# Four cross-attention layers in one kernel: recurrent read-outs and group-norm root on GpSimd, the tail of the grouped-query stage moved into the next stage, and weights loaded in another order

## The chip, the cores and the metric

One core of one Trainium2 chip runs the whole program; the other cores are idle. The metric is the device time of one launch in microseconds (us). The engines are TensorE (PE), VectorE (DVE), ScalarE (ACT), GpSimd (POOL) and SyncE (SP), which issues nearly all DMAs. Every engine runs a program of its own, written out by hand, and they meet only at semaphores.

## What is computed

Four layers in a row work on `x`, 4 batches of 256 tokens by 256 channels in f32, against a context of the same shape. Cut to what matters here:

```python
# L0: 16-head cross attention with a gate, then a layer norm on its input side
# L1: recurrent layer, 32 heads of 8 channels
def step(s, inp):
    k_l, v_l, w_l, r_l = inp
    a = k_l[..., :, None] * v_l[..., None, :]
    out = einsum('bhs,bhst->bht', r_l, faaaa * a + s)      # the read-out
    return a + w_l[..., None] * s, out
_, outs = lax.scan(step, s0, seq)
y = outs.transpose(1, 0, 2, 3)
gm = mean(y, -1); gv = mean((y - gm) ** 2, -1)             # group norm over 8 channels
y = ((y - gm) * rsqrt(gv + EPS)).reshape(B, L, C) * gn_w + gn_b
x = x + y * g @ Wo.T                                       # then the channel mix on top
# L2: grouped-query attention, 32 query heads on 8 key heads
x = out @ Wo + bo + x
x = (x - mean(x)) * rsqrt(var(x) + EPS) * gamma + beta     # the tail of the stage
# L3: two 16-head cross attentions of width 128 with a bias key and value, then an MLP
```

## The kernel before, in words

The program is a chain of five stages, joined by a barrier (`meet` on each engine, `lead` on SP, L295 to L310): an engine that has finished drains itself (L297), reports, and goes on when SP has heard all five.

**Stage 0, `stacked_first` (L605), layer L0.** Work goes in 8 steps (two per batch, 8 heads each) of 8 chunks. Keys and queries are split into three bf16 parts (`split0` L560, three GpSimd passes), written to DRAM (`keep_keys0` L528, `keep_queries0` L534) and read back with the heads laid out over 72 rows (`spread0` L541: two DMAs at L550 and two at L556). `spread0(m)` serves step m; PE's score products (L634) of a step wait for both. The maxima of the scores of a step are turned on PE (L674), copied by ACT (L830) and sent by a small DMA that ACT issues (L832); the flips of scores (L649) of the step wait for it, since the landed maxima are rows of the same product. SP's order is written out in `stacked0_sp` (L570): spreads, keeps, and at chunks 6 and 7 of a step two entries each of the table `later` (L2787), which loads what the later stages need: `rows` (the row constants of all layers, written to all 128 partitions, 1152 KB), the small and the large weights of L1 (`layer1`, 256 KB for each of r, k, v, g, o, fk, fr, fv) and those of L2. As a filler PE projects, in stages 0 and 1, context keys and values of L3 ahead (L1074, L1077), ACT copies them (L1088, L1090), and SP stores them (L1100, L1111).

**Stage 1, `rwkv_block` (L1733), layer L1, four rounds (one per batch).** In each, DVE runs a loop of 8 steps j: a scan in two halves (L2313), the next product of key and value (L2296, one operand from PE's banks), and the read-out product `rT * state` (L2322), which PE sums over groups of channels (L1937) and turns (L1946). There are two `state` buffers and four `read` buffers; a scan j >= 2 waits for read-out j-2. After the loop DVE adds the bonus (L2328), takes mean and variance of each head (L2334 to L2340), waits for ACT's root (L2131, `Sqrt`, which has its table loaded first), inverts it (L2342), refines it with one Newton step (L2344 to L2347), and scales, weighs and gates y (L2349, L2352, L2353). Then PE turns y for the output product. POOL makes three inputs (L2190), the gated weights (L2193, L2195), the bonus product (L2199), and ends the channel mix of the batch before (`finish_tail`, L2177 and L2179). In round 3 it also splits keys and queries of stage 2 (`split_into` L1168: L1170, L1172, L1174, twice), which SP keeps in DRAM (L1190, L1197) before it loads the kept keys of L3 (L1207) that free ACT's buffers.

**Stage 2, `stacked_attention` (L1300), layer L2.** It starts with POOL clearing and filling padded value tiles (`v_pad`, L1582, L1587, semaphore `pad_ready`). Its last batch ends with the output product on PE (L333), DVE's sum with x and bias (L1672, L1677), statistics (L247, L253, L255), POOL's root (L272, `pow` with exponent -0.5 on 128x2), DVE's centring (L265), and POOL's gamma and beta (L1574, L1576); only then do POOL and DVE report to the barrier.

**Stage 3, `wide_stream` (L2401), the two 16-head attentions,** 128 items in one software pipeline: per item PE's scores (L2422), DVE's maximum (L2576), ACT's exponential (L2516), DVE's division (L2584), PE's flips (L2432), PE's weighing (L2456), DVE's copy (L2590) and PE's output product (`add_head`, L2466, into bank J1). **Stage 4, `mlp` (L2647).**

The few lines that the names above stand for:

```python
if n < 1:                                          # L584, in stacked0_sp
    sp.wait_ge(max0_rows_ready, n + 2)
    spread0(sp, n + 3)
later = {0: [table] + layer1[8:11], 1: layer1[11:15], ..., 5: layer1[0:4], 6: layer1[4:8]}
act.activation(root, var, ACT.Sqrt)                # L2131
pool.tensor_tensor(relu, relu, rr, ALU.mult)       # L2177, finish_tail
pool.tensor_tensor(x_of(b), x_of(b), relu, ALU.add)
```

## Time and profile before

| | us |
|---|---|
| median of 3 runs (1333.21, 1333.27, 1338.27) | 1333.27 |
| the profiled execution's own time | 1336.37 |
| its span | 1334.6 |
| stage 0 | 0 to 197.0 |
| stage 1, rounds 0 to 3 | 197.0, 254.3, 318.2, 381.0 to 481.7 |
| stage 2 | 481.7 to 754.4 |
| stage 3 | 754.4 to 1272.0 |
| stage 4 | 1272.0 to 1334.6 |
| PE, DVE, ACT, POOL busy | 1229.8, 807.0, 536.7, 180.2 |

The times of the stages are places in the span, read from the timeline. A row of a timeline gives start, duration, engine, line, operation, output and input, shape and count, and in brackets the idle time before it with what ended that. The chain of waits is followed back from the last instruction. Durations in the rows below come from this one execution, whose own time is 3.1 us over the median.

### The profile page before, as it was taken

Reading aid. Unit: us, or ns where it says so; the run is one execution under the profiler, and the core shown is the slowest. Engines: PE = TensorE matmul, PEld = TensorE weight load, DVE = VectorE, ACT = ScalarE, POOL = GpSimd, SP = SyncE. Lnnn points to the kernel's source line nnn. Section 1 sums busy time; section 2 is a strip of 40 time slices with the busy share of each in tenths; the row PEclk is TensorE's granted clock in tenths of the full one; section 3 lists DMA queues with packets and bytes.
Section 4 is the critical chain, followed back from the end, with each engine's and each line's share of the span. In section 5 each row is a group of like instructions: output and inputs, shape, how many; then the busy total and the mean of one; then the engine's idle time right before and its main releaser. Section 6 shows DMA issues by size and latency. Waiting matters only on the chain.

```text
span 1334.6 us, 17906 instructions
## 1 busy us (share of the span) xinstructions
PE 1229.8 (92%) x6056; PEld 862.5 (65%) x6064; DVE 807.0 (60%) x2386; ACT 536.7 (40%) x1233; POOL 180.2 (13%) x397
## 2 busy tenths in 40 slices
PE   7769788898989787999999699999999999999999
PEld 4347555464555343444443488888888888888887
DVE  4434337586958336787785466666666666666620
ACT  3235343343534324555455343344343434334432
POOL 3122013022212111102011100000000000000000
PEclk9779899899989879999999899999999999999999
DMA  7454623101111535543524733030303030500000
GB/s 224 129 146 127 199 74 117 71 32 64 40 56 49 151 134 153 175 130 118 170 77 140 255 130 119 9 127 0 127 0 127 0 127 0 190 1 1 1 9 24
DMA packets 100652, 127.59 MB, mean 96 GB/s; under 512 B 6737, under 2 KB 78577, under 8 KB 98321
## 3 DMA queue, kind: packets, MB, share of 16 engines
q1 hardware_dynamic: 99936, 126.14, 29.1%
q8 instruction: 49, 0.80, 0.3%
q10 hardware_dynamic: 624, 0.30, 0.1%
q14 instruction: 43, 0.34, 0.1%
HBM read 79.33 MB, written 46.79 MB: 95 GB/s over the span
## 4 chain that ended last, share of the span: by engine, by line
PE 77%; DMA 8%; DVE 5%; ACT 3%; SPq 2%; issue 2%; POOL 2%; ACTq 0%; POOLq 0%; DVEq 0%
PE J L2448 8%; PE J L2466 8%; PE TT L2456 8%; PE S L2422 4%; PE OO L1077 4%; PE TT L2432 4%; PE OO L2422 4%; PE OO L1074 3%; PE J L324 2%; PE J L1077 2%; PE J L1343 2%; PE OO L2666 2%; PE S L634 2%; DMA km<-query_parts 2%; PE J L1074 2%
## 5 line engine op out<-in xcount | busy, mean ns | idle before, releaser
L2524 ACT ACTIVATE PT<-TT 128x512 f32<-128x512 f32 x128 | 76.5, 597 | 281.2 <-PE TT L2432 281.2
L2595 DVE TENSOR_SCALAR QK<-J,cols 128x256 f32<-128x256 f32 x126 | 61.0, 484 | 69.6 <-PE J L2448 69.6
L2559 POOL COPY On<-probs 128x8 f32<-128x8 f32 x128 | 29.1, 227 | 475.3 <-DVE probs L2584 446.0
L2584 DVE TENSOR_SCALAR probs<-probs,inv 128x257 f32<-128x257 f32 x256 | 79.1, 352 | 4.5
L1077 PE MATMUL OO<-ctxT,weights_a 128*128 128x512 f32 x136 | 69.9, 638 | 12.3 <-SPq L308 9.5
L2432 PE MATMUL TT<-ident,probs 128*128 128x128 f32 x512 | 76.9, 273 | 1.7 <-DVE probs L2584 1.7
L1074 PE MATMUL OO<-weights_a,ctxT 128*128 128x512 f32 x136 | 67.8, 622 | 9.8 <-SPq L308 6.1
L2432 PEld LDWEIGHTS TT<-ident,probs 128*128 128x128 f32 x512 | 63.8, 141 | 15.7 <-DVE probs L2584 3.0
L2590 DVE COPY km<-TT 128x256 f32<-128x256 f32 x128 | 54.2, 423 | 31.0 <-PE TT L2456 30.8
L970 DVE CUSTOM_DVE_ANT_0 mask_b<-S,weights_a 128x256 f32<-128x256 f32 x64 | 24.6, 422 | 70.0 <-PE S L634 69.8
L2576 DVE TENSOR_REDUCE maxes<-S 128x1 f32<-128x257 f32 x128 | 48.4, 420 | 30.4 <-PE S L2422 30.4
L2466 PE MATMUL J<-early,km 128*128 128x256 f32 x256 | 65.8, 379 | 0.3 <-DVE km L2590 0.3
L2456 PE MATMUL TT<-PT,early 128*128 128x256 f32 x256 | 65.9, 380 | 0.0
L2456 PE MATMUL TT<-PT,weights_a 128*128 128x256 f32 x256 | 65.8, 379 | 0.0
L2466 PE MATMUL J<-weights_a,km 128*128 128x256 f32 x256 | 65.6, 379 | 0.0
L1624 DVE CUSTOM_DVE_ANT_0 mask_b<-S,early 128x256 f32<-128x256 f32 x128 | 48.7, 418 | 27.9 <-PE S L1313 27.8
L2576 DVE TENSOR_REDUCE maxes<-OO 128x1 f32<-128x257 f32 x128 | 48.5, 421 | 26.4 <-PE OO L2422 25.5
L2516 ACT ACTIVATE probs<-S,maxes 128x257 f32<-128x257 f32 x128 | 59.4, 474 | 8.7 <-DVE maxes L2576 8.7
L2313 DVE TENSOR_TENSOR_SCAN early<-km,early 128x256 f32<-128x256 f32 x64 | 57.3, 935 | 6.0 <-issue 6.0
L2516 ACT ACTIVATE probs<-OO,maxes 128x257 f32<-128x257 f32 x128 | 59.3, 473 | 0.1
L2456 PEld LDWEIGHTS TT<-PT,early 128*128 128x128 f32 x256 | 48.5, 190 | 7.0 <-ACT PT L2524 0.4
L2456 PEld LDWEIGHTS TT<-PT,weights_a 128*128 128x128 f32 x256 | 48.6, 190 | 6.8 <-ACT PT L2524 0.2
(413 smaller groups left out, 2704.4 us busy)
## 6 DMA issues: line engine op xcount, KB each, us to landing
wide_keys<-weights_a SPq DMA_DIRECT2D x64, 256.0 KB, 2.1
wide_values<-weights_a SPq DMA_DIRECT2D x56, 256.0 KB, 2.0
query_parts<-weights_a SPq DMA_DIRECT2D x48, 192.0 KB, 2.8
weights_a<-wide_keys SPq DMA_DIRECT2D x16, 512.0 KB, 7.2
weights_a<-wide_values SPq DMA_DIRECT2D x16, 512.0 KB, 8.4
early<-wide_keys SPq DMA_DIRECT2D x16, 512.0 KB, 8.2
early<-wide_values SPq DMA_DIRECT2D x16, 512.0 KB, 8.7
weights_a<-key_parts SPq DMA_DIRECT2D x16, 288.0 KB
```

Of the source, the lines that this page charges most:

```text
L1074: mm = pe.matmul(bank_[:, :], ctxT[:, k, b * S + t * P:b * S + (t + 1) * P], values_, start=(k == 0), stop=(k == KC - 1))
L1077: mm = pe.matmul(bank_[:, :], ahead_k[a][:, k, h * P:(h + 1) * P], ctxT[:, k, pair * 512:pair * 512 + 512], start=(k == 0), stop=(k == KC ...
L2422: mm = pe.matmul(L_[n % 2][qt][:, 0:T], QK[:, n % 2, 0, qt * P:(qt + 1) * P], kept[g % 2][0][:, h, :], start=True, stop=True)
L2432: mm = pe.transpose(T0[:, st * S + qt * P:st * S + (qt + 1) * P], P_[n % 2][:, qt, st * P:(st + 1) * P], ident[:, :])
L2448: mm = pe.matmul(J0[:, 0:S], wide[a][0][:, k, h * P:(h + 1) * P], hidden[g % 2][:, k, :], start=(k == 0), stop=(k == KC - 1))
L2456: mm = pe.matmul(T1[:, 0:S], kept[g % 2][1][:, st, h * P:(h + 1) * P], PT[:, n % 2, st * S:(st + 1) * S], start=(st == 0), stop=(st == TQ ...
L2466: pe.matmul(J1[:, qt * S:(qt + 1) * S], avT[:, n % 2, qt * P:(qt + 1) * P], wide[a][1][:, h, :], start=(h == 0 and qt == 0), stop=False)
L2516: ins = act.activation(P_[n % 2][:, qt, 0:T], L_[n % 2][qt][:, 0:T], ACT.Exp, bias=maxes[:, qt, n % 32:n % 32 + 1], accum_out=sums[:, qt, ...
L2524: act.activation(PT[:, n % 2, :], T0[:, :], ACT.Copy).then_inc(pt3_ready, 1)
L2576: ins = dve.tensor_reduce(maxes[:, qt, n % 32:n % 32 + 1], L_[n % 2][qt][:, 0:T], AX_X, ALU.max, negate=True)
L2584: ins = dve.tensor_scalar(P_[n % 2][:, qt, :], P_[n % 2][:, qt, :], inv[:, qt, n % 32:n % 32 + 1], None, ALU.mult)
L2595: dve.tensor_scalar(QK[:, n % 2, 0, 0:S], J0[:, 0:S], head_cols(f"bq{a + 1}")[:, h:h + 1], float(DIM3) ** -0.5, ALU.add, ALU.mult).then_in ...
```

## The change

**In stage 1** the 8 read-out products of a round move from DVE to POOL, where the three passes for gated weights and bonus product now stand between them (after j = 2, 3 and 5); and the group-norm root is taken by POOL as `var ** -0.5` on 128x64 in one pass, in place of ACT's `Sqrt`, DVE's reciprocal and the four Newton passes. In POOL's order it stands after the read-outs and ahead of `finish_tail` and, in round 3, of the splits.

**In stage 0** `spread0(3)` follows `spread0(2)` at once, and the table `rows` is loaded in step 5 in place of step 0; the entries of `later` shift with it, two of the large weights from step 6 to step 7, and L2's output weight from step 3 to step 5.

**Stage 2** no longer waits for the padding on PE, nor on DVE before its first values; and the tail of its last batch moves into stage 3: the output product goes to bank J1, DVE adds x and bias ahead of the first maximum, takes statistics at the end of item 0 and centres in item 1, POOL takes the root in item 1, gamma in item 2, beta in item 3; PE's first output product of stage 3 waits until DVE has read J1, and DVE waits for beta in item 7.

The diff, without most of its context:

```diff
@@ -581,9 +581,11 @@
                 if i == 5 and 0 <= n + 1 < STEPS0:
-                    if n < 1:
+                    if n < 0:
                         sp.wait_ge(max0_rows_ready, n + 2)
                         spread0(sp, n + 3)
+                if at == 1:
+                    spread0(sp, 3)
                 if n >= 0 and i >= 6:
@@ -1432,7 +1434,6 @@
 
-                pe.wait_ge(pad_ready, 1)
                 for at in range(-LEAD2, LAST):
@@ -1468,7 +1469,7 @@
                 project_head(pe, 0, 1, 1)
-                project_out(B - 1, O0)
+                project_out(B - 1, J1)
                 bias_rows_pe(pe, 0, S0)
@@ -1608,8 +1609,6 @@
                 bias_rows_pool(pool, 0)
-                root(B - 1)
-                scale_out(B - 1)
                 meet(pool, "pool")
@@ -1683,7 +1682,6 @@
 
-                dve.wait_ge(pad_ready, 1)
                 for at in range(-LEAD2, LAST):
@@ -1693,6 +1691,7 @@
                     if at == 2 - LEAD2:
+                        dve.wait_ge(pad_ready, 1)
                         fetch_values(0)
@@ -1715,10 +1714,6 @@
                 fetch_q(dve, 0, 1, 1)
-                add_out(B - 1, O0)
-                add_bias()
-                variance()
-                centre_out(B - 1)
                 meet(dve, "dve")
@@ -2127,8 +2122,6 @@
                     late(0)
-                    act.wait_ge(gvar_ready, 1)
-                    act.activation(root, var, ACT.Sqrt).then_inc(groot_ready, 1)
                     late(1)
@@ -2189,16 +2182,28 @@
                             .then_inc(xf_ready, 1)
-                    pool.wait_ge(g_ready, 1)
-                    pool.tensor_tensor(gated_w, silu_g, row("L1_xattn_gn_w").unsqueeze(1).to_broadcast([P, TQ, C]),
-                                       ALU.mult)
-                    pool.tensor_tensor(gated_b, silu_g, row("L1_xattn_gn_b").unsqueeze(1).to_broadcast([P, TQ, C]),
-                                       ALU.mult).then_inc(gates_ready, 1)
-                    pool.wait_ge(v_ready, 1)
-                    pool.wait_ge(bonus_ready, 1)
-                    pool.tensor_tensor(tmp3, v_tok[:, :, :].rearrange("p t (h j) -> p (t h) j", j=DIM1),
-                                       bonus.unsqueeze(2).to_broadcast([P, TQ * HEADS1, DIM1]), ALU.mult)\
-                        .then_inc(bonus_times_v, 1)
+                    pool.wait_ge(r_ready, 1)
+                    for j in range(DIM1):
+                        pool.wait_ge(state_ready, j + 1)
+                        if j >= 4:
+                            pool.wait_ge(y_done, (j - 4) // 2 + 1)
+                        pool.tensor_tensor(read[j % 4], rT, state[j % 2][:, :, 0:S], ALU.mult).then_inc(read_ready, 1)
+                        if j == 2:
+                            pool.wait_ge(g_ready, 1)
+                            pool.tensor_tensor(gated_w, silu_g, row("L1_xattn_gn_w").unsqueeze(1).to_broadcast([P, TQ, C]),
+                                               ALU.mult)
+                        if j == 3:
+                            pool.tensor_tensor(gated_b, silu_g, row("L1_xattn_gn_b").unsqueeze(1).to_broadcast([P, TQ, C]),
+                                               ALU.mult).then_inc(gates_ready, 1)
+                        if j == 5:
+                            pool.wait_ge(v_ready, 1)
+                            pool.wait_ge(bonus_ready, 1)
+                            pool.tensor_tensor(tmp3, v_tok[:, :, :].rearrange("p t (h j) -> p (t h) j", j=DIM1),
+                                               bonus.unsqueeze(2).to_broadcast([P, TQ * HEADS1, DIM1]), ALU.mult)\
+                                .then_inc(bonus_times_v, 1)
+                    pool.wait_ge(gvar_ready, 1)
+                    pool.tensor_tensor(root, var, halves[:, 0:1].to_broadcast([P, TQ * HEADS1]), ALU.pow)\
+                        .then_inc(groot_ready, 1)
                     if b_before is not None:
@@ -2316,10 +2321,6 @@
                             times_k(j + 1)
-                        dve.wait_ge(state_ready, j + 1)
-                        if j >= 4:
-                            dve.wait_ge(y_done, (j - 4) // 2 + 1)
-                        dve.tensor_tensor(read[j % 4], rT, state[j % 2][:, :, 0:S], ALU.mult).then_inc(read_ready, 1)
 
@@ -2339,12 +2340,6 @@
                     dve.wait_ge(groot_ready, 1)
-                    chain.link(dve.reciprocal(root, root))
-
-                    chain.link(dve.tensor_tensor(mean, root, root, ALU.mult))
-                    chain.link(dve.tensor_tensor(mean, mean, var, ALU.mult))
-                    chain.link(dve.tensor_scalar(mean, mean, -0.5, 1.5, ALU.mult, ALU.add))
-                    chain.link(dve.tensor_tensor(root, root, mean, ALU.mult))
                     wide_rstd = root.unsqueeze(2).to_broadcast([P, TQ * HEADS1, DIM1])
@@ -2385,6 +2380,8 @@
         h3_flipped, h3_ready, weights_cleared = names3("h3_flipped"), names3("h3_ready"), names3("weights_cleared")
+        last2_read, last2_var, last2_rstd, last2_normed, last2_step, last2_scaled = (names3(n) for n in (
+            "last2_read", "last2_var", "last2_rstd", "last2_normed", "last2_step", "last2_scaled"))
         FRONT_AT = 8
@@ -2462,6 +2459,8 @@
                         pe.wait_ge(out3_fetched, g)
+                    if n == 0:
+                        pe.wait_ge(last2_read, 1)
                     for qt in range(TQ):
@@ -2560,6 +2559,16 @@
                         take_root(pool, next_rstd.rearrange("p t o -> p (t o)"), var3_ready, rstd3_ready, g + 1)
+                    if n == 1:
+                        take_root(pool, own_rstd.rearrange("p t o -> p (t o)"), last2_var, last2_rstd, 1)
+                    if n == 2:
+                        gamma = row("L2_xattn_gamma").unsqueeze(1).to_broadcast([P, TQ, C])
+                        pool.wait_ge(last2_normed, 1)
+                        pool.tensor_tensor(xn[:, :, :], xn[:, :, :], gamma, ALU.mult).then_inc(last2_step, 1)
+                    if n == 3:
+                        beta = row("L2_xattn_beta").unsqueeze(1).to_broadcast([P, TQ, C])
+                        pool.wait_ge(last2_step, 1)
+                        pool.tensor_tensor(x_of(B - 1), xn[:, :, :], beta, ALU.add).then_inc(last2_scaled, 1)
                     if n == HEADS3:
@@ -2605,6 +2614,10 @@
 
+                bo2 = row("L2_xattn_bo").unsqueeze(1).to_broadcast([P, TQ, C])
+                dve.tensor_tensor(xn[:, :, :], two(J1), x_of(B - 1), ALU.add).then_inc(last2_read, 1)
+                dve.wait_ge(last2_read, 1)
+                chain.link(dve.tensor_tensor(xn[:, :, :], xn[:, :, :], bo2, ALU.add))
                 maxima(0)
@@ -2621,6 +2634,13 @@
                         add_out(g - 1)
+                    if n == 0:
+                        take_stats(dve, chain, lambda t: xn[:, t, :])
+                        take_variance(dve, chain, EPS2, own_rstd, last2_var)
+                    if n == 1:
+                        centre(dve, lambda t: xn[:, t, :], xn, own_rstd, last2_rstd, 1, last2_normed)
+                    if n == 7:
+                        dve.wait_ge(last2_scaled, 1)
                     following = x_tok, (g + 1) % B
@@ -2784,9 +2804,10 @@
                      .to_broadcast([P, len(ROWS), C]))
-            later = {0: [table] + layer1[8:11], 1: layer1[11:15], 2: layer1[15:17],
-                     3: [(w[n], n, "w2", split_k(d[n])) for n in ("L2_q", "L2_k", "L2_v", "L2_o")],
-                     5: layer1[0:4], 6: layer1[4:8]}
+            later = {1: layer1[8:12], 2: layer1[12:16],
+                     3: [layer1[16]] + [(w[n], n, "w2", split_k(d[n])) for n in ("L2_q", "L2_k", "L2_v")],
+                     5: [(w["L2_o"], "L2_o", "w2", split_k(d["L2_o"])), table] + layer1[0:2], 6: layer1[2:6],
+                     7: layer1[6:8]}
 
@@ -2794,7 +2815,7 @@
                         sp.wait_ge(ahead_done, FIRST)
-                    if name == "L1_r":
+                    if name == "L2_o":
                         for stored_ in ahead_stored:
```

SyncE, early in stage 0, before, from the spread of step 2 (`key_parts_0` and `query_parts_0` are the split parts in DRAM; a row of L2755 is a load from the table `later`):

```order
L550 DMA weights_a<-key_parts_0 72x1x2048 x2
L556 DMA early<-query_parts_0 72x2048 x2
L531 DMA key_parts_0<-weights_a 128x3x256 x2
L550 DMA weights_a<-key_parts_0 72x1x2048 x2
L556 DMA early<-query_parts_0 72x2048 x2
L2755 DMA rows<-in_rows 128x2304
L2755 DMA early<-in_L1_w1 128x2x160
L2755 DMA early<-in_L1_dec1 128x2x64
L2755 DMA early<-in_L1_dec2 64x256
L538 DMA query_parts_0<-weights_a 128x3x256 x6
L550 DMA weights_a<-key_parts_0 72x1x2048 x2
L556 DMA km0<-query_parts_0 72x2048 x2
```

The same place with the change (the loads' line is now L2775):

```order
L550 DMA weights_a<-key_parts_0 72x1x2048 x2
L556 DMA early<-query_parts_0 72x2048 x2
L550 DMA weights_a<-key_parts_0 72x1x2048 x2
L556 DMA early<-query_parts_0 72x2048 x2
L531 DMA key_parts_0<-weights_a 128x3x256 x2
L538 DMA query_parts_0<-weights_a 128x3x256 x6
L550 DMA weights_a<-key_parts_0 72x1x2048 x2
L556 DMA km0<-query_parts_0 72x2048 x2
L2775 DMA early<-in_L1_w1 128x2x160
```

The second spread (step 3) went ahead of the keeps, and four loads that stood ahead of the queries' keep (L538) are behind the spread of step 4 or, `rows`, at the end of the stage. There SyncE now has, behind the stores of the first values:

```order
L2775 DMA early<-in_L2_o 128x2x256
L2775 DMA rows<-in_rows 128x2304
L2775 DMA early<-in_L1_r 128x2x256
L2775 DMA early<-in_L1_k 128x2x256
L2775 DMA early<-in_L1_v 128x2x256
L2775 DMA early<-in_L1_g 128x2x256
L2775 DMA early<-in_L1_o 128x2x256
L2775 DMA early<-in_L1_fk 128x2x256
L2775 DMA early<-in_L1_fr 128x2x256
L2775 DMA early<-in_L1_fv 128x2x256
```

Before, the eight loads of L1 stood there alone. GpSimd in round 3 of stage 1, before, from the three inputs on (`weights_a` of 128x256 and 128x512 are the splits; the pair L2177, L2179 is the tail of the batch before):

```order
L2190 TENSOR_TENSOR km0<-masked,hT 128x512 x3
L2193 TENSOR_TENSOR km0<-early,rows 128x512
L2195 TENSOR_TENSOR km0<-early,rows 128x512
L2199 TENSOR_TENSOR probs<-V,QK 128x512
L2177 TENSOR_TENSOR weights_a<-weights_a 128x512
L2179 TENSOR_TENSOR x_tok<-x_tok,weights_a 128x512
L1170 TENSOR_TENSOR weights_a<-weights_a 128x256
```

and with the change (L2190 is now the read-out, L2205 the root, L2170 and L2172 the tail, L1172 the first split):

```order
L2183 TENSOR_TENSOR km0<-masked,hT 128x512 x3
L2190 TENSOR_TENSOR early<-km0,early 128x512 x2
L2190 TENSOR_TENSOR km0<-km0,early 128x512
L2193 TENSOR_TENSOR km0<-early,rows 128x512
L2190 TENSOR_TENSOR km0<-km0,early 128x512
L2196 TENSOR_TENSOR km0<-early,rows 128x512
L2190 TENSOR_TENSOR early<-km0,early 128x512 x2
L2201 TENSOR_TENSOR probs<-V,QK 128x512
L2190 TENSOR_TENSOR km0<-km0,early 128x512 x2
L2205 TENSOR_TENSOR QK<-QK,halves 128x64
L2170 TENSOR_TENSOR weights_a<-weights_a 128x512
L1172 TENSOR_TENSOR weights_a<-weights_a 128x256
```

Eight read-outs and the root are new on GpSimd, and the tail and the splits stand behind the root.

## Rows read from the trace of the kernel before

**Rows 1.** The page, chain that ended last: shares of the span by engine.

```profile
PE 77%; DMA 8%; DVE 5%; ACT 3%; SPq 2%; issue 2%; POOL 2%; ACTq 0%; POOLq 0%; DVEq 0%
```

**Rows 2.** Busy time by stretch: length, PE, PEld, DVE, ACT, POOL busy, PEclk, DMA share, GB/s.

```profile
0.00:197.00 197.00, 154.67 (x1028) 105.07 (x1028) 79.52 (x329) 73.46 (x129) 36.49 (x89) 0.87 0.51 151
754.40:1272.00 517.60, 514.70 (x2663) 449.48 (x2664) 331.02 (x964) 205.47 (x665) 36.23 (x145) 1.00 0.21 70
```

**Rows 3.** Timeline of PE, 52 to 112 us.

```profile
90.17 1.04 PE L634 MATMUL S<-weights_a,early 72*128 72x256 bf16 x4 [10.82 <-DMA early<-query_parts]
```

**Rows 4.** Timeline of SP's queue, 50 to 100 us.

```profile
76.29 0.37 SPq L2755 DMA_DIRECT2D rows<-in_rows  x1
...
82.71 10.74 SPq L538 DMA_DIRECT2D query_parts<-weights_a  x6
```

**Rows 5.** Chain of waits, 50 to 182 us, in order of time: start, us, what.

```profile
92.97 3.95 DMA query_parts<-weights_a
97.31 12.19 DMA km<-query_parts
109.54 0.61 PE S L634 x4
...
144.91 9.48 DMA km<-weights_a
...
180.37 0.45 PE OO L649 x4
```

**Rows 6.** Busy time of two stretches of stage 0; columns as in rows 2.

```profile
90.00:94.00 4.00, 3.83 (x19) 2.96 (x20) 1.55 (x8) 0.69 (x1) 0.00 (x0) 0.50 0.57 178
144.00:156.00 12.00, 7.79 (x64) 5.71 (x62) 3.61 (x18) 3.87 (x7) 0.00 (x0) 0.94 0.98 286
```

**Rows 7.** Timelines of SP's queue and of ACT's, end of stage 0.

```profile
167.07 0.38 SPq L2755 DMA_DIRECT2D early<-in_L_r  x1
...
175.66 0.73 ACTq L832 DMA_DIRECT2D early<-weights_a  x1
```

**Rows 8.** POOL by line and shape, 190 to 485 us: count, busy us, mean ns, idle before.

```profile
L272 POOL TENSOR_TENSOR rstd<-rstd,halves 128x2 f32<-128x2 f32 x7 | 4.9, 700 | 38.8 <-DVE rstd L255 38.8
```

**Rows 9.** Timeline of all engines, round 3: DVE beside the two tail passes of POOL.

```profile
427.06 1.74 POOL L2177 TENSOR_TENSOR weights_a<-weights_a 128x512 f32<-128x512 f32 x1 [10.30 <-ACT weights_a L2046]
427.60 3.37 DVE L2313 TENSOR_TENSOR_SCAN early<-km,early 128x256 f32<-128x256 f32 x2
```

**Rows 10.** Timelines of DVE and PE, round 0, the last steps of the loop.

```profile
237.43 1.39 DVE L2313 TENSOR_TENSOR_SCAN early<-km,early 128x256 f32<-128x256 f32 x2
238.85 0.69 DVE L2322 TENSOR_TENSOR km<-km,early 128x512 f32<-128x512 f32 x1
...
241.46 0.64 PE L1937 MATMUL OO<-km,head 128*32 128x256 f32 x8
```

**Rows 11.** Timeline of DVE, 309 to 318.2 us: the tail of round 1.

```profile
313.69 0.20 DVE L2340 TENSOR_SCALAR QK<-QK 128x64 f32<-128x64 f32 x1
...
315.80 0.69 DVE L2349 TENSOR_TENSOR probs<-probs,QK 128x512 f32<-128x512 f32 x1
```

**Rows 12.** Timelines of DVE and POOL, round 3's tail, 436 to 449 us.

```profile
440.83 0.30 DVE L2340 TENSOR_SCALAR QK<-QK 128x64 f32<-128x64 f32 x1
...
438.86 0.67 POOL L1170 TENSOR_TENSOR weights_a<-weights_a 128x256 f32<-128x256 f32 x1 [8.44 <-ACT weights_a L1153]
...
443.49 1.15 POOL L1174 TENSOR_TENSOR weights_a<-weights_a 128x512 bf16<-128x512 f32 x1
```

**Rows 13.** Chain of waits in round 3's tail, and PE's timeline at the start of stage 2.

```profile
447.09 0.37 SPq L1197
...
483.50 1.03 PE L1313 MATMUL S<-early,weights_a 72*128 72x256 bf16 x4 [3.83 <-POOL early L1587]
```

**Rows 14.** End of stage 2: PE's last work in its timeline, POOL's drain in the chain.

```profile
747.04 1.93 PE L456 MATMUL S<-weights_a,mask_b 128*32 128x256 f32 x32
...
752.77 1.37 POOLq L297
```

## The prediction

> **What bounds the kernel now.** I read the chain's shares first: TensorE holds 77% of the path, DMA 8%, DVE 5% and POOL 2% [rows 1]. So moving work between DVE and POOL pays only where PE stands still behind one of them. The stretches say where that is [rows 2]: in stage 0 PE works 154.7 of 197 us, in stage 3 it works 514.7 of 517.6, so nothing added there is free unless it fits beside PE. Then I went to the places that the diff touches. In stage 0 PE stands 10.82 us for the spread of step 3 [rows 3], which SP issued with the 1152 KB table close behind it [rows 4]; the chain then runs over the keep and the spread of step 4, which lands at 109.5 after 12.19 us, and later over a maxima DMA of 12 KB that took 9.48 us in the thick of other transfers [rows 5]. In stage 1 the loop's read-outs arrive just in time for PE [rows 10], and the tail is a serial string on DVE [rows 11], which in round 3 ends in a string on SP [rows 13]. At the end of stage 2 everyone waits for POOL [rows 14].
>
> **Stage 1, the loop.** Each step had on DVE a scan pair of 1.39 and the read-out of 0.69 [rows 10], and a product from PE's banks of the same width, about 0.65. The read-out on POOL takes about what POOL's other 512-wide pass takes, 1.15 us [rows 12]. Does it run beside the scan? The trace has one clear case: two POOL passes (1.74 and about 1.5) under one pair of scans, which took 3.37 instead of 1.39 [rows 9]. Almost the whole of the POOL time was added. So I count scan and read-out in turn, 2.6 a step with the PE-bank product hidden, and the three old POOL passes (about 1.1 each) also in turn: 8 x 2.6 + 3.3 = 24.1 us from the first scan to the last read-out, where 8 x 2.73 made 22. In round 0 PE takes its last group at 241.46, and the last read-out ended at 239.5 [rows 10]: two spare microseconds, used up. In rounds 1 to 3 the read-outs come just ahead of PE as now. I take 0.25 a round, **+1.0** in all (from 0, if PE's filler hides it, to +8, the whole 2.1 four times).
>
> **Stage 1, the root.** From the variance (end of L2340 at 313.89) to the first scaling (315.80) DVE spends 1.91 us on ACT's root, the reciprocal and Newton's steps [rows 11]. In their place stands one POOL pass of length p plus 0.1 to hand over. In round 0, which has no tail of a batch before, that is p - 1.8. In rounds 1 and 2 `finish_tail` now follows the root, so its two passes fall on DVE's last three (3 x 0.69) instead of into the loop. A scan pair lost 2.0 to them [rows 9]; I take 2.3 for three passes, so p + 0.5 each. In round 3 the splits stand behind root and tail. The variance is there at 441.1, the splits last 5 us or so (438.86 to 444.64 with a gap) [rows 12]; root, tail beside DVE (3.2) and splits end at 449.2 + p, while SP needed them at 447.09 and the chain runs on from there through the keeps [rows 13]: p + 2.1. Together **4p + 1.3**.
>
> **What is p?** No row shows `pow` on 128x64. On 128x2 it takes 0.70 [rows 8]. The low end lets it grow as a plain pass does, 62 more elements at 1.15 / 512 us [rows 12]: 0.84. The high end lets every element cost the same 0.35: 22.4. These are far apart. I take p = 1.5, near the low end, since the nearest row is the same operation and part of its 0.70 must be its start; it allows `pow` some 13 ns an element, six times a plain pass. So 4p + 1.3 = **+7.3**.
>
> **Stage 0, the early spread.** With `spread0(3)` right behind `spread0(2)` its 10.82 us wait goes [rows 3]. Late next is the spread of step 4. Its keep (L538) took 10.74 to issue behind the table [rows 4]. Without it six issues at about 0.45 end at 85.5, land 3 to 4 us later (3.95 in the chain), and the spread lands 12.19 after that [rows 5]: 100.9 in place of 109.54, -8.6. But PE now reaches that wait about 7 us early. After the old stall the granted clock was 0.50 [rows 6], the 1.2 GHz level, and the same four score products took 1.04 [rows 3] in place of 0.61 [rows 5]. That slow stretch was swallowed before, since PE then waited for the spread anyway, and is paid now behind it: about 8 us of work at half speed, +3.5. The next maxima DMA now travels behind a second spread, +1. Sum -4.1.
>
> **Stage 0, the late burst.** Behind the last values SP used to issue eight loads from 167.07 on [rows 7], 2.1 MB with the other stage 0 traffic done. Now 256 KB for L2 and the 1152 KB table stand ahead of them, 3.5 MB. At the 286 GB/s of the crowded stretch from 144 to 156 [rows 6] that lasts 12 us, to 179; at a tenth less, to 181. The maxima DMA of step 7 is issued at 175.66 [rows 7] and PE needs it at 180.37 [rows 5]; today it travels alone. Under load the same 12 KB took 9.48 [rows 5]. So 175.66 + 9.48 = 185.1, 4.8 late, less what the earlier gain shifts, with no more than half a microsecond of clock: **+4**. (The Trainium skill, "DMA: Bandwidth & Descriptors", section "Queues, rings and completion order", has each engine take turns between the queue rows it has work for, a packet at a time, by which ACT's small transfer would hardly wait behind SP's backlog. By that rule this term would be nothing and the sum 4 us lower.) The 9.48 us of the chain speak against the rule as a promise of time. Small shifts of the other loads: -0.4. Stage 0 in all **-0.5** (from -9 to +7).
>
> **The seam between stages 2 and 3.** PE need no longer wait for POOL's clearing, which held it from the barrier at 482.0 to 483.50 [rows 13]: **-1.5**. At the end the barrier waited for POOL's drain until 754.14; PE's last work ends at 748.97, and ACT copies it in about 0.4 [rows 14]: **-4.7**. What moved has a price in stage 3, where PE is busy 99% [rows 2]. DVE's two additions (0.69 each, as its other 512-wide passes [rows 11]) lie under PE's first scores; statistics and centring, some 2 us together, fall into two items, and DVE has (517.6 - 331.0) / 128 = 1.46 idle in each [rows 2]; POOL is free, and the waits of PE and of DVE in item 7 find their work long done. I take **+0.7** (0 to 3).
>
> **Sum.** 1.0 + 7.3 - 0.5 - 1.5 - 4.7 + 0.7 = +2.3 us. The profiled execution's own time is 1336.4, so 1338.7 by it; that execution stands 3.1 over the median of the runs, so against the median 1333.3 I say **1335.6**. About 0.5%, 6.7 us, is what a measurement of this kernel can tell from no change, so this is no change.
>
> **Rivals.**
> - *`pow` is paid by the element (slower).* The place is the 128x64 pass between variance and scaling, four times, with DVE idle behind it and PE soon after. The sum is 4p - 3.7. It decides from p = 2.6 on. At p = 5 it is +16, 1350; at 16 it is +60, 1394. For it: in a plain pass two elements are nothing, so most of the 0.70 on 128x2 [rows 8] is `pow`'s own, and if none of that is start it grows thirtyfold. Against it: only that the fixed part is unknown. Chance 0.27.
> - *The burst wins (slower).* The table and L2's weight collide with both late maxima DMAs, the loop locks as at [rows 9] in every round, and p stays small: stage 0 +7, loops +5, together +14, 1347. One crowding in two places; chance 0.07.
> - *Stage 0 keeps its gain (faster).* The clock holds since the idle is shorter than 10.82, the maxima pass the loads: -8.6 + 0.5, and with p = 0.84, where POOL and DVE also share better than at [rows 9], the total is -8.1 + 0.5 + 2.7 - 5.5 = -10.4, 1323. Chance 0.23.
> - *The change doesn't do what it says.* The wait for spread 3 goes, and the one for spread 4 stays at 109.5 because the split queries, not the table, held L538. But the row of L538 begins at 82.71 only when the split is there, and it is its 10.74 us for six issues that is long [rows 4]. If it stays so, stage 0 is +4 and the total +7, 1340. Counted half with the forecast, half with slower.
>
> (The Trainium skill, "SBUF — State Buffer", section "SBUF: two separate sides", calls the port pair that DVE and GpSimd share an exclusive lock, taken for a whole instruction, for DVE operations with two SBUF inputs against GpSimd operations that read SBUF; by it the pairing of read-out and scan would be in turn everywhere, and the loop's price at its full length.) The 3.37 of [rows 9] agrees. What keeps my loop term at +1.0 is PE's slack, not sharing.
>
> **How the numbers follow.** Forecast 0.43, within 0.5%. Slower: 0.27 of `pow`, 0.07 of the burst, rounded, **0.34**. Faster: **0.23**. The range reaches down to the third rival, 1323, and up through `pow` at p of about 6 (+20), 1354; what lies outside is mostly a `pow` of 8 us and more, 0.15, and a little below.
>
> **What would show it.** Right: the row of `pow` on 128x64 near 1.5 us with DVE waiting 1.6 behind L2341; DVE's scans longer than 0.72 a half where a read-out lies over them; the 10.82 us wait gone and a new wait at the first products of step 4 near 94 to 101; a wait of PE's flips of step 7 behind ACT's DMA near 182; stage 2 some 6 us shorter. Wrong: a `pow` row above 2.6 us, PE's idle in stage 0 below 35 us, or stage 3 longer by more than 3 us.

## The result and the profile after

The changed kernel takes 1373.16 us (median of 4 runs, 1367.90 to 1375.14) against 1335.77 for the kernel before in the same measurement (the three runs of the table above and a fourth, 1340.93). The ratio, new time over that of the kernel before, is 1.0277, 95% interval 1.0248 to 1.0306. The profiled execution's own time is 1373.1, 36.7 over that of before. The kernel is slower, and its time lies above the range, which ended at 1354. Ratios below are to the kernel before as well, measured beside each experiment, since its median moves between 1331.8 and 1337.1.

The page after: the busy times, for POOL's, and the chain's shares by engine, to be held against [rows 1].

```profile
PE 1237.1 (90%) x6056; PEld 867.2 (63%) x6064; DVE 793.6 (58%) x2334; ACT 529.3 (39%) x1224; POOL 259.4 (19%) x433
...
PE 71%; DMA 9%; issue 5%; POOL 5%; DVE 5%; ACT 2%; SPq 2%; POOLq 1%; ACTq 0%; DVEq 0%
```

POOL is busy 79 us more, and POOL, its queue and "issue" have taken from PE's share. The groups of POOL by line and shape, 150 to 520 us, answer to [rows 8]:

```profile
L2205 POOL TENSOR_TENSOR QK<-QK,halves 128x64 f32<-128x64 f32 x4 | 42.1, 10530 | 38.0 <-DVE QK L2341 38.0
L2190 POOL TENSOR_TENSOR early<-km,early 128x512 f32<-128x512 f32 x16 | 18.9, 1184 | 46.5 <-DVE early L2318 46.5
```

The `pow` pass on 128x64 takes 10.53 us, seven times the value I had taken; a read-out takes 1.18, as forecast. Round 1's tail in the timelines of DVE, POOL and PE, against [rows 11]:

```profile
318.54 0.20 DVE L2341 TENSOR_SCALAR QK<-QK 128x64 f32<-128x64 f32 x1
329.37 1.74 DVE L2344 TENSOR_TENSOR probs<-probs,QK 128x512 f32<-128x512 f32 x1 [10.64 <-POOL QK L2205]
```

```profile
318.81 10.53 POOL L2205 TENSOR_TENSOR QK<-QK,halves 128x64 f32<-128x64 f32 x1 [9.67 <-DVE QK L2341]
329.31 1.26 POOL L2170 TENSOR_TENSOR weights_a<-weights_a 128x512 f32<-128x512 f32 x1
```

```profile
333.97 2.92 PE L1079 MATMUL OO<-ctxT,weights_a 128*128 128x512 f32 x3 [15.45 <-SPq L308]
```

DVE waits 10.64 us for the root, where it had 1.91 of work in its place. Its first scaling then takes 1.74 in place of 0.69, since the batch tail has just started on POOL. PE stands for 15.45 us at the end of the round. The chain of waits names the pass in rounds 1 to 3 ("POOL QK L2205", 2% of the span on the page). In round 0 it does not:

```profile
246.22 10.57 POOLq L297
```

The 10.57 us put down to POOL's drain (L297) are the `pow` pass, which POOL's timeline has from 246.26 for 10.53. The groups by line and shape count all four passes.

Where the time went, by the places where POOL starts each part (its first clearing of stage 1, its copy of the start column in each round, its clearings at the start of stages 2 and 3, the end of the span), in us:

```
                   stage 0   round 0  round 1  round 2  round 3   stage 2   stages 3, 4
before              197.5     57.2     63.9     62.8    100.6      272.7      579.9
changed             194.1     65.6     74.5     73.3    113.8      267.8      582.3
difference           -3.4     +8.3    +10.7    +10.5    +13.2       -5.0       +2.4
```

Stage 1 has lost 42.7 us, everything else together gained 6.0. Each row is one execution; how far such numbers carry is said below the table of the experiments.

### The profile page after: what moved, and what is told of

Read it like the earlier page. It is cut to its first block, busy times and chain, and to the rows that moved or that the text cites. A ratio compares the mean times of both kernels' runs of the same rounds, so it can differ in the third digit from the quotient of the medians.

```text
span 1371.3 us, 17886 instructions
## 1 busy us (share of the span) xinstructions
PE 1237.1 (90%) x6056; PEld 867.2 (63%) x6064; DVE 793.6 (58%) x2334; ACT 529.3 (39%) x1224; POOL 259.4 (19%) x433
## 4 chain that ended last, share of the span: by engine, by line
PE 71%; DMA 9%; issue 5%; POOL 5%; DVE 5%; ACT 2%; SPq 2%; POOLq 1%; ACTq 0%; DVEq 0%
PE J L2445 8%; PE TT L2453 8%; PE J L2465 8%; PE TT L2429 4%; PE OO L1079 4%; PE S L2419 4%; PE OO L2419 4%; PE OO L1076 4%; POOL QK L2205 2%; PE J L324 2%; DMA km<-query_parts 2%; PE J L1345 2%; PE OO L2686 2%; DMA early<-query_parts 2%; PE S L324 1%
## 5 line engine op out<-in xcount | busy, mean ns | idle before, releaser
L1076 PE MATMUL OO<-weights_a,ctxT 128*128 128x512 f32 x136 | 72.3, 658 | 17.4 <-SPq L308 14.8
L2318 DVE TENSOR_TENSOR_SCAN early<-km,early 128x256 f32<-128x256 f32 x64 | 64.8, 1052 | 10.9 <-ACT early L2088 10.1
L1079 PEld LDWEIGHTS OO<-ctxT,weights_a 128*128 128x128 f32 x136 | 24.2, 197 | 62.0 <-issue 54.3
```

Of the source, the lines that this page charges most:

```text
L1076: mm = pe.matmul(bank_[:, :], ctxT[:, k, b * S + t * P:b * S + (t + 1) * P], values_, start=(k == 0), stop=(k == KC - 1))
L1079: mm = pe.matmul(bank_[:, :], ahead_k[a][:, k, h * P:(h + 1) * P], ctxT[:, k, pair * 512:pair * 512 + 512], start=(k == 0), stop=(k == KC ...
L2318: ins = dve.tensor_tensor_scan(state[j % 2][:, half, 1:S + 1], wT[:, half, :], kv[j % 2][:, half, :], start[:, half, j:j + 1], ALU.mult, A ...
```

## Experiments

The same division of the span for the kernels of e2 to e15, one profiled execution each ("stage 1" is the sum of the four rounds):

```
                          stage 0  stage 1  stage 2  stages 3, 4
e2 recurrent part only     193.6    325.8    273.9     581.6
e3 the other part only     196.0    281.9    265.8     579.2
e4 change, old root        193.3    278.6    265.8     579.2
e5 batch tail first        192.9    318.9    266.0     579.2
e6 root only               193.3    326.8    272.8     579.8
e7 read-outs only          194.7    282.7    273.5     581.9
e8 seam only               192.9    279.7    266.3     579.2
e9 stage 0 part only       194.5    282.2    272.4     581.5
e10 early spread only      197.4    284.4    272.0     581.5
e11 late table only        190.4    281.6    272.0     581.6
e12 half of the root       192.6    303.6    265.3     579.1
e13 as e4                  197.2    282.4    266.8     582.3
e14 e4 without stage 0     195.4    279.2    265.9     579.2
e15 as e3                  197.6    285.7    267.2     579.2
```

One execution differs from the next by a few us in the same code: stage 1 without the new root runs from 278.6 to 285.7, stage 0 unchanged from 192.9 to 197.5, stages 3 and 4 from 579.1 to 582.3. So a column is read over all kernels that share the code of that stage.

In stage 1 and in stages 3 and 4 this goes with TensorE's granted clock. It stood at the 1.2 GHz level for 20.5 us of stage 1 in e8 and e14 (279.7 and 279.2 long), for 33.5 us in e15 (285.7). Stages 3 and 4 with the seam part of the change take 579.1 or 579.2 in the seven executions that spend no time there at that level, and 582.3 in the two (the changed kernel and e13) that spend 6.8 us, half of it near the head of stage 3 and half at the head of stage 4. The first 20 us of stage 3 in the changed kernel and in e8, columns as in [rows 2], the granted clock third from the right:

```profile
789.00:809.00 20.00, 17.44 (x80) 14.81 (x81) 13.53 (x41) 7.06 (x24) 4.62 (x11) 0.91 0.99 337
739.00:759.00 20.00, 17.61 (x89) 14.71 (x90) 13.93 (x44) 7.28 (x24) 4.70 (x12) 1.00 0.99 340
```

**e1, what `pow` costs by itself.** The passes stand at the end of POOL's program in the kernel before:

```diff
+pool.memset(probe, 1.7).then_inc(probe_ready, 1)
+pool.wait_ge(probe_ready, 1)
+for rows_, width, op in ([(P, n, ALU.pow) for n in (2, 8, 16, 32, 64, 128)] +
+                         [(P, 2, ALU.mult), (P, 64, ALU.mult), (32, 64, ALU.pow)]):
+    pool.tensor_tensor(probed[0:rows_, at:at + width], probe[0:rows_, 0:width],
+                       halves[0:rows_, 0:1].to_broadcast([rows_, width]), op)
```

> The kernel before, with nine extra POOL passes at the end of POOL's program in the MLP stage, where POOL is idle: pow on 128 partitions by 2, 8, 16, 32, 64 and 128 elements, a plain multiplication on 128x2 and 128x64, and pow on 32x64. Their results are not used. Theory (pow is paid by the element, with a small start): 0.70, 1.65, 2.9, 5.5, 10.5 and 20.7 us, that is 0.158 us an element over 0.38; the multiplications 0.2 and 0.35 us; 32x64 as long as 128x64 if partitions work in parallel. Rival (the 10.5 us in the changed kernel came from waiting on VectorE, which shares the port): the probe's 128x64 is near 1.5 to 3 us, since VectorE is nearly idle here.

POOL by line and shape, from 1272 us on (columns as in [rows 8]; a group of two holds the `pow` and the multiplication of that width):

```profile
L2721 POOL TENSOR_TENSOR PT<-masked,halves 128x128 f32<-128x128 f32 x1 | 20.7, 20721 | 0.0
L2721 POOL TENSOR_TENSOR PT<-masked,halves 128x64 f32<-128x64 f32 x2 | 10.8, 5400 | 0.0
L2721 POOL TENSOR_TENSOR PT<-masked,halves 32x64 f32<-32x64 f32 x1 | 10.5, 10506 | 0.0
L2721 POOL TENSOR_TENSOR PT<-masked,halves 128x32 f32<-128x32 f32 x1 | 5.4, 5410 | 0.0
L2721 POOL TENSOR_TENSOR PT<-masked,halves 128x16 f32<-128x16 f32 x1 | 2.9, 2890 | 0.0
L2721 POOL TENSOR_TENSOR PT<-masked,halves 128x2 f32<-128x2 f32 x2 | 0.9, 442 | 0.1
```

From 16 elements of the free size (those of one partition) on it is a line: (20.72 - 2.89) / 112 = 0.159 us an element, over a start of some 0.35. The pair at 128x64 sums to 10.8, so the multiplication there takes 0.3 and `pow` 10.5; at 128x2 the multiplication takes about 0.2 and `pow` 0.7. A quarter of the partitions costs the same. With VectorE nearly idle it is 10.5 still: the rival, that the pass waits on VectorE at the shared port, falls. The whole time, 1346.43, says nothing, since the passes outlast the MLP.

**e2 and e3, the two parts.** e2 has the diff's recurrent hunks alone, e3 all the others.

```diff
 # e2, against before (rwkv_block alone):
-dve.tensor_tensor(read[j % 4], rT, state[j % 2][:, :, 0:S], ALU.mult).then_inc(read_ready, 1)
+pool.tensor_tensor(read[j % 4], rT, state[j % 2][:, :, 0:S], ALU.mult).then_inc(read_ready, 1)
-act.activation(root, var, ACT.Sqrt).then_inc(groot_ready, 1)
+pool.tensor_tensor(root, var, halves[:, 0:1].to_broadcast([P, TQ * HEADS1]), ALU.pow)
 # ... (reciprocal and Newton passes go as well)
 # e3, against the change: these same lines taken back
```

> Only the recurrent part of the change (read-outs and root on POOL), stage 0 and stages 2 and 3 as before. Theory: stage 1 alone carries the loss, and by the difference of the rounds in the two traces (8.3, 10.7, 10.5 and 13.2 us) it is +42.7, so about 1378 by the median of before of 1335.8. Rival (the recurrent rounds wait for the weights that the other part loads later): with the loads back in their old places stage 1 grows by clearly less, +30 or so, 1366.

> Only the other part (early spread, late table, padding wait, tail of stage 2 in stage 3), stage 1 as before. Theory: stage 0 -3.4, stage 2 -5.0, stages 3 and 4 +2.4, in all -6.0, about 1330, at the bound of what can be told from no change. Rival (late weights hurt the recurrent rounds): 1336 or more, with a wait for a DMA at the head of round 0.

e2 takes 1375.78, ratio 1.0287 (1.0236 to 1.0338), and e3 1323.46, ratio 0.9889 (0.9831 to 0.9946). The whole loss is in the recurrent part. The later weights hurt no round: stage 1 takes 281.9 in e3 and 284.5 before. e2 agrees with the theory. e3 gained 6.5 us more than the 1330 expected; e15 measures it again.

**e4, the change with the old root.**

```diff
-pool.tensor_tensor(root, var, halves[:, 0:1].to_broadcast([P, TQ * HEADS1]), ALU.pow)
+act.activation(root, var, ACT.Sqrt).then_inc(groot_ready, 1)     # then, on DVE:
+chain.link(dve.reciprocal(root, root))
...
```

> The changed kernel with the read-outs still on POOL, but the group-norm root taken as before: ACT's Sqrt, DVE's reciprocal and the four Newton passes. Theory (the pow pass is the loss, 10.6 against 1.9 us of path four times): 8.7 x 4 = 35 us off 1373, about 1338; stage 1 then within some 7 us of before. Rival (read-outs on POOL and their contention with the scans are the loss): not over 10 us off, 1363 or more.

1320.03, ratio 0.9880 (0.9826 to 0.9934): 53 us off the changed kernel and 1.2% below the one before. The read-outs stay on POOL in it, so their contention is not the loss. The expected 1338 was 18 us too high. Stage 1 alone shrinks by 48.6 in the traces: 4 x 8.7 left out the passes queued behind the root, which e5 puts at some 7 us. e13 repeats the kernel, with 44.8.

**e5, the batch tail ahead of the root.**

```diff
+if b_before is not None:
+    finish_tail(b_before, 1)
 pool.wait_ge(gvar_ready, 1)
 pool.tensor_tensor(root, var, ..., ALU.pow).then_inc(groot_ready, 1)
-if b_before is not None:
-    finish_tail(b_before, 1)
```

> The changed kernel with POOL's finish_tail ahead of the root in place of behind it (POOL is idle there for some 9.7 us before the root, so the two passes find room). Theory (the prediction's ordering term, two passes on DVE's last three): the first of those three takes 0.69 in place of 1.74 in rounds 1 to 3, and round 3's splits start 2.8 us earlier; -1 to -2.3 in rounds 1 and 2, -3 in round 3, together -5 to -7, 1367. Rival (the port is shared without loss at that place): less than 2 us.

In the trace stage 1 falls from 327.2 to 318.9, 8.3 us, which by itself is hardly more than the scatter. The stretch from the end of the variance to the start of the next part scatters less: in rounds 1 to 3 it takes 13.42, 13.43 and 51.92 us where the changed kernel has 15.41, 15.42 and 55.03, together 7.1 less. DVE's first scaling in round 1 (timeline of DVE) is back at its length:

```profile
326.55 0.69 DVE L2344 TENSOR_TENSOR probs<-probs,QK 128x512 f32<-128x512 f32 x1 [10.64 <-POOL QK L2207]
```

The whole time is 1362.65; its ratio to before, 1.0246 (1.0177 to 1.0315), is too wide to tell it from the change by itself. The ordering term is shown by the rows, not by the ratio.

**e6 and e7, root alone and read-outs alone on POOL,** each in the kernel before.

```diff
 # e6, POOL, after bonus_times_v; read-outs (L2322) stay on DVE; ACT's and DVE's part of the root goes
+pool.tensor_tensor(root, var, halves[:, 0:1].to_broadcast([P, TQ * HEADS1]), ALU.pow)
 # e7, POOL's loop as changed; root by ACT and DVE as before
+pool.tensor_tensor(read[j % 4], rT, state[j % 2][:, :, 0:S], ALU.mult).then_inc(read_ready, 1)
```

> The kernel before with the root alone on POOL (pow on 128x64), read-outs and everything else as before. Theory (pow is the whole loss): 4 x (10.6 - 1.9) = 35, and 2.3 for each of rounds 1 and 2 and 4 in round 3 for the passes queued behind it: +43 at most, 1372 to 1380 against 1337. Rival (the loss needs both, root and read-outs together on POOL): under +25.

> The kernel before with the read-outs alone on POOL, root on ACT and DVE as before. The prediction's loop term says +1.0. The traces of the changed kernel with the old root say -5.9 in stage 1 against before, of which the version without read-outs on POOL already had -2.6, so -3.3 from the read-outs: 1334. Rival (contention of scan and read-out costs up to the full length): +4 to +8.

e6: 1378.77, ratio 1.0349 (1.0297 to 1.0402). The root alone costs all of it: 40 to 54 us of whole time, and 42.3 in stage 1 of the traces. e7: 1330.20, ratio 0.9981 (0.9962 to 1.0001): the read-outs are worth 0 to 5 us, a gain if anything. Its round 0 is 55.7 long, as in e4, e13 and e14, which share it, against 57.2 or more in all that have neither read-outs nor root on POOL. The reason is in the trace. In round 0 of the kernel before, PE waits for DVE's fourth read-out:

```profile
230.11 0.64 PE L1937 MATMUL OO<-km,head 128*32 128x256 f32 x8 [1.74 <-DVE km L2322]
```

POOL's passes for the gated weights and the bonus product (222.19 to 227.03) had stretched the third scan pair to 3.38 us and the third read-out to 1.33. With the read-outs on POOL only the first of these three passes stands ahead of the fourth read-out, and this wait is gone in every kernel with the new loop (e2, e4, e7, e13, e14) and there, 1.73 or 1.74 us, with the old one (e6, for one). So it is the new place of the three passes, moved by the same edit, that gains it, as far as the traces tell; no run moves them alone.

**e8, the seam of stages 2 and 3 alone** (padding wait, and tail moved into stage 3).

```diff
-pe.wait_ge(pad_ready, 1)
-project_out(B - 1, O0)
+project_out(B - 1, J1)
...
```

> The kernel before with the padding wait and the tail of stage 2 moved as in the change, stages 0 and 1 as before. Theory (the prediction's terms -1.5, -4.7 and +0.7): -5.5, 1331.5. What the traces say with the other part in it: stage 2 -7.0, stages 3 and 4 -0.7: -7.7, 1329. Rival (the gain of the seam is given back by stage 3, whose items are PE-bound): within 2 us of before.

1327.25, ratio 0.9959 (0.9934 to 0.9984), so -5.5 (-2.1 to -8.8): the prediction's sum of the three terms.

**e9 to e11, the stage 0 part, whole and in halves.**

```diff
 # e9: both; e10: the first alone; e11: the second alone
-if n < 1:                # around spread0(sp, n + 3)
+if n < 0:
+if at == 1:
+    spread0(sp, 3)
-later = {0: [table] + layer1[8:11], ...}
+later = {1: layer1[8:12], ..., 5: [(w["L2_o"], ...), table] + layer1[0:2], ...}
 # ...
```

> The kernel before with the stage 0 part alone: the early spread of step 3 and the table and weights loaded later. The prediction's sum says -0.5 (-4.1 for the spread, +4 for the burst). The three traces with this part start round 0 at 193.3 to 196.0, before and a version with stage 0 as before at 193.6 and 197.5, so the traces alone leave -1.3 as a mean, with 2 to 4 us between executions. Measurement of whole times: version with both seam and stage 0 -12 to -14, seam alone -5, so the rest gives stage 0 -7 to -8. I expect -4, 1328. Rival (nothing but scatter of the spreads' transfers): within 2 us.

> Only the early spread of step 3, the table where it was, now between the spreads' issues and the queries' keep. Theory (the 10.8 us wait of step 3 goes, but the table still stands before the keep and the spread of step 4, so the wait moves there): within 2 us of before, with a wait of 8 to 12 us at the first product of step 4. Rival (the spread is what counts): -4 and more.

> Only the loads moved (table to step 5, weights shifted), the spread of step 3 where it was. Theory (the keep and spread of step 4 come earlier, the stall of step 3 stays): about 0 to -3, the wait of step 3 still 8 to 10 us; a wait behind ACT's maxima DMA of step 7 appears, +2. Rival (the burst at the end costs 4 or more): slower than before by 2 to 4.

The ratios are 1.0003 (0.9978 to 1.0029), 0.9994 (0.9969 to 1.0020) and 0.9982 (0.9957 to 1.0007). My -4 for e9 was wrong, and the prediction's -0.5 lies inside e9's interval of -2.9 to +3.9 us. The column agrees: stage 0 takes 194.8 on average in the eight executions with both halves and 194.6 in the six without. What PE waited for, 60 to 190 us (total, times, longest), first e10, then e11:

```profile
PE S L636 <- DMA km<-query_parts: 5.8, 1, 5.8
PE S L636 <- DMA early<-query_parts: 2.5, 1, 2.5
```

```profile
PE S L634 <- DMA early<-query_parts: 10.4, 3, 8.5
```

With the early spread the 10.8 us wait is gone and one of 5.8 stands at step 4, shorter than the 8 to 12 expected; with the late table alone it stays, at 8.5. The wait behind ACT's maxima DMA of step 7, put at 2 us for e11, is 0.4 there.

**e12, half of the root.** The kernel leaves out the normalisation of the other 32 head columns.

```diff
-pool.tensor_tensor(root, var, halves[:, 0:1].to_broadcast([P, TQ * HEADS1]), ALU.pow)
+pool.tensor_tensor(root[:, 0:32], var[:, 0:32], halves[:, 0:1].to_broadcast([P, 32]), ALU.pow)
```

> The changed kernel with the root taken on POOL for the first 32 of the 64 head columns only; the other 32 are scaled by what stands there, so y of half of the heads is not normalised. Theory (the pow pass lies on the path at its full length, and is paid by the element): the pass takes 5.4 in place of 10.5 us, so 4 x 5.1 = 20.4 off, 1352.5. Rival (part of it is hidden by PE's fill-in work): 10 or less.

```profile
L2205 POOL TENSOR_TENSOR QK<-QK,halves 128x32 f32<-128x32 f32 x4 | 21.7, 5424 | 38.0 <-DVE QK L2341 38.0
```

1346.53, ratio 1.0101 (1.0056 to 1.0147). Stage 1 is 23.6 shorter than in the change, where 4 x 5.1 = 20.4 were expected; the 3 us more are within what stage 1 differs between executions. From the end of the variance to the next part it takes 5.1 us less in each of rounds 0 to 2, the whole 5.1 by which the pass is shorter, and 6.3 in round 3. Nothing of the pass is hidden.

**e13 to e15, what is left without the new root, again.** e13 is e4, e15 is e3, and e14 is e4 with stage 0 as before:

```diff
 # e14, against e13
-if n < 0:                # around spread0(sp, n + 3)
+if n < 1:
-if at == 1:
-    spread0(sp, 3)
-later = {1: layer1[8:12], ...}
+later = {0: [table] + layer1[8:11], ...}
 # ...
```

> The same kernel as e4: the change with the old group-norm root. Theory (parts add: seam -5.5, read-outs -2.5, stage 0 0): -8, ratio 0.994. Rival (together they give what the first measurement showed): -16, ratio 0.988.

> The kernel before with the seam and the read-outs on POOL, old root, and stage 0 as before. Theory (stage 0's part is worth nothing): same as e13 within 2 us. Rival (the gain of e3 and e4 over the seam alone came from stage 0's part): slower than e13 by 5 or more.

> The same kernel as e3: seam and stage 0 part, stage 1 as before. Theory (parts add): -5.5, ratio 0.996. Rival: 0.989 as first measured.

e13: 1322.87, ratio 0.9913 (0.9893 to 0.9934). e14: 1322.34, ratio 0.9927 (0.9897 to 0.9957). e15: 1327.93, ratio 0.9964 (0.9942 to 0.9987). So e13 and e14 cannot be told apart, and the stage 0 part is worth nothing that these runs can tell. e15 is the seam's 5. The first measurement of e3 is not repeated. Its four runs had a granted clock of 0.963 to 0.968, e15's twelve, of the same program, 0.955 to 0.965; why the clock differed is open. Between e15 and e13 lie 5 us, and the read-outs are the only difference between them (e7 alone: 0 to 5). The version with seam and read-outs, and the old root, beats the kernel before by 0.7 to 0.9% and the changed kernel by some 3.5%.

## Why the prediction was wrong, step by step

**The root.** The step that failed is "I take p = 1.5, near the low end", p being the length of the `pow` pass on 128x64. Measured, p is 10.53 us, so the term 4p + 1.3, put at +7.3, is +43.4 by its own formula. The formula held. From the end of the variance to the start of the next part it took 4.71, 4.69, 4.70 and 40.86 us before, and 13.43, 15.41, 15.42 and 55.03 with the change:

```
             forecast at p = 10.53    measured
round 0           + 8.7                + 8.7
round 1           +11.0                +10.7
round 2           +11.0                +10.7
round 3           +12.6                +14.2
```

The sum with this p is 1.0 + 43.4 - 0.5 - 1.5 - 4.7 + 0.7 = +38.4, and the measured difference is +36.7 in the profiled executions and +37.4 in the medians. That this meets within 2 us is partly luck: the rounds in the table sum to +44.3, the loop was no loss, and a single execution scatters by as much. So the first rival came true (chance 0.27), with its place, its way of counting and its point of decision at 2.6 us. The reason for taking 1.5, that part of the 0.70 on 128x2 must be a start, was true of half of it: 0.35 us. The argument that I put into the rival was the better one and could have been finished with rows at hand. POOL's shortest passes in the same trace take 0.2 us (a copy of 128x8), so about 0.5 of the 0.70 was `pow`'s own on two elements. If the share f of that is paid by the element, the pass takes 0.7 + 15.5 f at 64. A p of 1.5 needs f = 0.05, nearly all of `pow`'s own time a start as well, for which no row spoke; an even guess of f = 0.5 gives 8.5. Measured, f is 0.63. The range ended at p = 6.

**The batch tail behind the root** was priced at 2.3 us a round with it and more in round 3: e5 takes back 2.0, 2.0 and 3.1 in rounds 1 to 3, 7.1 against 2.3 + 2.3 + 3.2 = 7.8 in my terms. Right.

**The loop** was given +1.0, by rounds in which scan and read-out go in turn, 24.1 us. POOL's and DVE's timelines in round 0:

```profile
216.58 1.19 POOL L2190 TENSOR_TENSOR early<-km,early 128x512 f32<-128x512 f32 x1 [5.73 <-DVE early L2318]
```

```profile
217.04 1.91 DVE L2318 TENSOR_TENSOR_SCAN early<-km,early 128x256 f32<-128x256 f32 x2
```

The read-out still has 0.72 us to go when the scan's row begins, and the scan pair takes 1.91 in place of 1.39, 0.52 more. The step of 2.52 us (217.04 to 219.56) is as long as before (2.48). From the first scan at 215.04 to the end of the last read-out at 237.63 it is 22.6 us where it was 22.1. So they go nearly in turn, as said, but a plain step takes 2.5 and not 2.6, and the three other passes add 0.7 to 1.0 each and not 1.1. What the prediction missed is that its "8 x 2.73" of before already held the three other passes, as one scan pair of 3.38 and one read-out of 1.33: plain steps took 2.48 there as well. Round 0, where the danger was seen, became 1.5 us shorter (e7), and e7 makes the whole 0 to -5: the term had the wrong sign by a few us at most. (The Trainium skill, "SBUF — State Buffer", section "SBUF: two separate sides", has the port pair that DVE and GpSimd share locked for a whole instruction.) These rows agree within 0.2 us: only the first half of the scan pair is longer (1.26 for 0.75), as if it had waited for the read-out's end, and the second takes its 0.72.

**The early spread.** PE's timeline, SP's queue and the chain after:

```profile
86.24 0.38 PE L676 MATMUL OO<-ident,weights_a 128*24 128x128 f32 x2 [2.67 <-POOL weights_a L928]
...
104.76 0.98 PE L636 MATMUL S<-weights_a,km 72*128 72x256 bf16 x4 [4.88 <-DMA km<-query_parts]
```

```profile
84.30 3.16 SPq L538 DMA_DIRECT2D query_parts<-weights_a  x6
```

```profile
86.93 4.48 DMA query_parts<-weights_a
91.81 12.90 DMA km<-query_parts
...
170.73 6.54 DMA early<-weights_a
```

The backlog was the cause of the slow keep: it issues in 3.16 in place of 10.74 us [rows 4]. But it takes the spread and the table together right ahead of it, and the prediction named the table. With the table in its old place and the spread of step 3 early (e10) the keep takes 3.17, without the table and with the spread where it was (e11) 4.88. The first product of step 4 comes at 104.76, 4.8 earlier instead of 8.6. Of the 3.8 us missing, the keep began 1.6 later and the two landings took 0.5 and 0.7 longer; the rest are short gaps that the forecast left out. It also put nothing on the spread of step 2, which now has the next one right behind it: PE waits 3.09 us for it where it waited 1.46 (3.45 in e9, 2.46 in e10). And the clock fell more than once:

```profile
88.00:92.00 4.00, 4.00 (x26) 2.43 (x19) 1.53 (x7) 2.25 (x4) 0.00 (x0) 0.50 0.47 124
104.50:108.50 4.00, 3.74 (x12) 3.03 (x13) 0.78 (x4) 0.00 (x0) 0.00 (x0) 0.57 0.25 81
```

(PEclk is the third value from the right.) PE runs at the 1.2 GHz level behind the 2.67 us wait for POOL and mostly again behind the 4.88 us wait for step 4. Before there was one slow stretch here, behind the one stall of 10.82 us [rows 6]. **The burst:** ACT's maxima DMA in the burst took 6.54, not 9.48, and PE waited 1.9 us for it, not 4; in e9 it waited 0.2. So both movements, put at 8.6 earlier and 4 later, were about half as large in this trace. They cancel, and e9 says 0 within 4 us. That the -0.5 came out is thus luck in part: neither of its two large terms was confirmed at its size.

**The seam.** Forecast -6.2 in stage 2 and +0.7 in stage 3. Over nine executions with it and seven without, stage 2 takes 266.3 and 272.8, -6.5. PE's wait at the head of the stage falls from 3.83 [rows 13] to 2.25, that at its end from 6.30 to 1.62:

```profile
755.27 2.05 PE L2422 MATMUL S<-weights_a,QK 128*128 128x257 f32 x4 [6.30 <-POOL early L2553]
789.59 1.10 PE L2419 MATMUL S<-weights_a,QK 128*128 128x257 f32 x4 [1.62 <-POOL early L2552]
```

The two rows, first before and then after, also show a gain that the prediction left out. Behind the long wait the granted clock was 0.52 (755.2 to 759.0), behind the short one 1.00 (789.5 to 793.3), and the first eight products of stage 3 took 3.72 and 1.97 us. So stages 3 and 4 take 579.9 and 581.1 with and without the seam, and the forecast +0.7 is not seen. Its price is one wait of PE at the head of stage 3, here from 788 us on:

```profile
PE TT L2429 <- DVE probs L2593: 2.0, 1, 2.0
```

Before, the longest wait of this kind was 1.1, so the price is 0.9. What would show the whole prediction wrong had been named: a `pow` row above 2.6 us. It was there.

## What to carry to other kernels

An operation that is slow on two elements may be paid by the element and not by the pass, as `pow` was here: measure it at the width at which it will be used, in an idle corner of the same program, before it goes on the path. A move between engines should be split: here the read-outs and the seam gained 10 us and one pass of 64 elements, four times, lost 45 behind them. Where two ends of a price differ by more than 25 times, the range has to hold the far one, or the forecast is of the price and not of the kernel.

## What the runs showed of the hardware

- `pow` on GpSimd takes 0.159 us an element of the free size over a start of 0.35 us, 10.5 us on 64, and the same on 32 partitions as on 128 (e1); a plain multiplication of 64 takes 0.3.
- The chain can show such a pass under the queue's drain: "POOLq L297" with 10.57 us in round 0. In the other three rounds it named the pass.
- From one execution to the next the same code of stage 0 takes within 5 us, of stage 1 within 7 and of the last two stages within 3.2, and in the last two this goes with how long TensorE's granted clock stands at its 1.2 GHz level (0 us: 579.2; 6.8 us: 582.3). A single pair of traces does not settle terms of this size; columns over many executions did.
- GpSimd's read-outs and DVE's scans, both reading SBUF, run nearly in turn (1.91 for 1.39 us), while DVE's product with one operand in PE's banks takes its usual 0.66 beside the same read-out.
